# First feed-forward layer: 23 expert blocks of dispatched rows in place of eight experts on all rows

## The reference

```python
x = x + L0_gnn(adj, layernorm(x))    # max over a node's first 25 neighbours, then a dense layer
x = x + L0_ffn(layernorm(x))         # 8 experts, hidden 512, two used for each row
x = x + L1_gnn(layernorm(x), adj)    # attention, 8 heads, masked by adj
x = x + L1_ffn(layernorm(x))         # 6 experts, hidden 128

# L0_ffn
top_w, top_i = top_k(xf @ Wg + bg, 2); top_w = softmax(top_w)
w_dense = sum(one_hot(top_i, 8) * top_w[..., None], axis=1)
for e in range(8):
    h = gelu(xf @ W1[e] + b1[e])
    out = out + w_dense[:, e:e + 1] * (h @ W2[e] + b2[e])
```

## Time and profile before

| | us |
|---|---|
| median of three runs | 3452.06 |
| the profiled execution | 3442.75 |
| its span, first to last instruction | 3440.9 |
| time around the span | 1.85 |
| mean granted TensorE clock | 0.901 of 2.4 GHz |
| busy: PE, DVE, ACT, POOL | 2589.0, 1840.7, 1292.2, 837.9 |

### The profile page before, as it was taken

The page is one execution under the profiler, slowest core; times in us unless marked ns, Lnnn a source line. Parts: engine busy times, 40 slices in busy tenths (PEclk is TensorE's granted clock), DMA queues, the critical chain, the costliest instruction groups (busy, mean ns, idle before and its releaser), DMA issues.

```text
span 3440.9 us, 48188 instructions
## 1 busy us (share of the span) xinstructions
PE 2589.0 (75%) x16137; PEld 1525.4 (44%) x16137; DVE 1840.7 (53%) x5404; ACT 1292.2 (38%) x1959; POOL 837.9 (24%) x917
## 2 busy tenths in 40 slices
PE   0018626997699878996799779995799789986697
PEld 0015423654365445554465445643465346543044
DVE  3224335843686357744685358734694379124903
ACT  1004212354334643264335433372335432452054
POOL 3533530433041502242042402252043400000000
PEclk9988867998899988998899889997899899997598
DMA  5523524422532433332542343242442241004100
GB/s 132 59 27 65 50 38 88 75 38 32 105 64 37 46 58 89 45 52 24 105 75 33 37 77 79 39 53 22 104 75 37 33 82 36 2 1 74 37 2 7
DMA packets 106030, 183.66 MB, mean 53 GB/s; under 512 B 19935, under 2 KB 56188, under 8 KB 105724
## 3 DMA queue, kind: packets, MB, share of 16 engines
q0 software_dynamic: 25344, 51.96, 17.5%
q1 hardware_dynamic: 80380, 128.07, 15.2%
HBM read 158.59 MB, written 20.97 MB: 52 GB/s over the span
## 4 chain that ended last, share of the span: by engine, by line
DVE 35%; PE 30%; issue 18%; DMA 7%; DVEq 5%; ACT 3%; SPq 1%; ACTq 0%
DVE parts L1034 15%; PE PH L1293 5%; PE PA L1339 5%; PE PY L1354 4%; PE PA L1342 4%; PE PY L1304 4%; DMA parts_dram<-parts 4%; DMA xn<-in_x 2%; DVE res_n L940 2%; ACT HB L1165 2%; DVE G L823 2%; DVEq L744 2%; DVE score L791 2%; DVE top L795 1%; DVE xn L773 1%
## 5 line engine op out<-in xcount | busy, mean ns | idle before, releaser
L716 POOL DMA_INDIRECT G<-table,slot_idx x792 | 811.4, 1024 | 372.8 <-issue 372.8
L1158 ACT ACTIVATE HB<-PH,bias_T 128x512 f32<-128x512 f32 x512 | 351.3, 687 | 862.4 <-PE PH L1293 862.4
L1034 DVE CUSTOM_DVE_ANT_0 parts<-PA,mask 128x1024 bf16<-128x1024 f32 x512 | 627.0, 1225 | 19.8 <-issue 19.8
L1165 ACT ACTIVATE HB<-PA 128x1024 f32<-128x1024 f32 x512 | 496.0, 1020 | 364.8 <-PE PA L1342 364.6
L1304 PEld LDWEIGHTS PY<-W_sb,HB 128*128 128x128 f32 x4096 | 512.3, 195 | 134.4 <-issue 87.9
L1304 PE MATMUL PY<-W_sb,HB 128*128 128x128 f32 x4096 | 521.3, 279 | 65.2 <-DVE res_n L940 53.7
L1293 PE MATMUL PH<-XT,W_sb 128*128 128x512 f32 x1024 | 527.0, 630 | 17.4 <-ACT HB L1158 17.4
L1316 PE MATMUL PA<-KS,QS 96*128 96x512 bf16 x1024 | 342.1, 420 | 114.2 <-DVE MX L1034 58.7
L1339 PE MATMUL PA<-QS,KS 99*128 99x512 bf16 x1024 | 393.6, 384 | 11.2 <-ACT HB L1165 7.4
L1342 PE MATMUL PA<-identb,mask 128*128 128x128 bf16 x4096 | 397.1, 218 | 0.0
L594 POOL TENSOR_TENSOR pool_pad<-pool_pad 1x1 f32<-1x1 f32 x112 | 23.6, 210 | 1520.4 <-DVE slot_idx L803 1275.0
(11 more groups left out here) (156 smaller groups left out, 2270.1 us busy)
## 6 DMA issues: line engine op xcount, KB each, us to landing
adj_sb<-in_adj SPq DMA_DIRECT2D x64, 512.0 KB, 4.2
adjm<-in_adj SPq DMA_DIRECT2D x64, 512.0 KB
G<-table,slot_idx POOLq DMA_INDIRECT x792
parts_dram<-parts SPq DMA_DIRECT2D x16, 768.0 KB, 6.9
QS<-parts_dram SPq DMA_DIRECT2D x48, 256.0 KB, 8.3
KS<-parts_dram SPq DMA_DIRECT2D x48, 256.0 KB, 8.1
xn<-in_x SPq DMA_DIRECT2D x8, 512.0 KB, 13.1
table<-xn SPq DMA_DIRECT2D x8, 512.0 KB, 3.5
```

Source lines behind the costliest of these rows:

```text
L716: pool.indirect_dma_start(G[:, t % 2, s, :], None, table, bass.IndirectOffsetOnAxis(slot_idx[:, t, s:s + 1], axis=0), bounds_check=ROWS - ...
L1034: ins = dve.tensor_tensor_reduce(out=junk, in0=psum(ps, step)[:, :], in1=mask[:, t, :], scale=1.0, scalar=LOWEST, op0=ALU.add, op1=ALU.max ...
L1158: act.activation(HB[:, i % 2, c, :], psum(ps, step)[:, :], ACT.Gelu, bias=bias_T[:, e * HC + c:e * HC + c + 1]).then_inc(*emptied(ps, step))
L1165: act.activation(HB[:, kc % 2, 2 * pr:2 * pr + 2, :], psum(ps, key)[:, :].rearrange("p (h q) -> p h q", h=2), ACT.Exp, scale=float(D) ** - ...
```

## The change

Rows are sent to their experts. The new step `rank` (PE and DVE) counts, after the two best experts of graph b+2 are known, how many rows each expert has, and gives each of the 2048 (row, choice) pairs a place in a list sorted by expert, in which each expert starts at a multiple of 128. `disp` has POOL write the rows there, with 16 indirect DMAs of 128 rows (`sorted_x` in DRAM). The list has at most 23 blocks of 128 rows, and always 23 are computed.

In the next pass, SP loads the sorted rows in groups of four blocks (`xs`), and PE transposes them (`xT`). For each block, SP reads the block's expert number into a register and loads that expert's weights, 128 x 1028 numbers (526 KB), into a ring of three buffers (`wl`). PE makes four 128x128 products, ACT four Gelus of 128 columns (`up`), and PE four products (`dn`). `yc` and `yst` bring a group's result back to DRAM. When all are stored, `comb` fetches two result rows for each row with 16 indirect DMAs on POOL, and DVE adds them with their weights (16 additions). `comb` stands behind `mT` and ahead of `st`. The two units behind `mparts` and `mT` and the last unit at the end are gone, as are all `acc0`. Blocks start in `weave` when its count of TensorE time reaches 22. Ahead of everything, SP writes 23 DMAs of zeros into `sorted_x`. POOL now walks the list of steps too.

```diff
-ORDER0 = [(hf, e) for hf in range(2) for e in range(E0)]
 FINDS_EARLY = 10
+BLOCKS = 2 * TILES + E0 - 1
+PER_GROUP = 4
+GROUPS = (BLOCKS + PER_GROUP - 1) // PER_GROUP
+WRING = 3
+BLOCKS_FROM = 22.0
+WCOLS = 2 * HID0 + HC
...
-UNITS_MIDDLE = 2
-UNITS_LATE = 1
...
-        elif scores and (len(emptied) < 2 or emptied[-2] <= tensor or not main):
+        elif scores and (len(emptied) < 2 or emptied[-2] <= tensor or not main or tensor < BLOCKS_FROM):
...
-            if main[0][0] == "acc0":
-                vector = max(vector, tensor) + 1.15
-            else:
-                tensor += 0.87
+            tensor += PACE.get(main[0][0], 0.0)
             s.append(main.pop(0))
...
+    blocks = []
+    if unit:
+        blocks += [("xs", 0), ("xs", 1)] + [("wl", j) for j in range(WRING)] + [("xT", 0)]
+        for j in range(BLOCKS + 1):
+            if j < BLOCKS:
+                if j % PER_GROUP == 2 and j // PER_GROUP + 1 < GROUPS:
+                    blocks.append(("xT", j // PER_GROUP + 1))
+                    if j // PER_GROUP + 2 < GROUPS:
+                        blocks.append(("xs", j // PER_GROUP + 2))
+                blocks.append(("up", j))
+            if j > 0:
+                blocks.append(("dn", j - 1))
+                if j - 1 + WRING < BLOCKS:
+                    blocks.append(("wl", j - 1 + WRING))
+                g, last = group_of(j - 1)
+                if last:
+                    blocks += [("yc", g), ("yst", g)]
...
+    joined = [("comb",)] if unit else []
+    if not att:
+        s += spread(blocks, finds) if blocks else finds
+        s += joined
     else:
         cut = FINDS_EARLY if finds else 0
-        s += weave(scores, main, finds[:cut]) + second[:1] + experts0(middle[:1])
-        s += second[1:2] + experts0(middle[1:])
+        s += weave(scores, blocks, finds[:cut]) + second[:2] + joined
         s += spread(second[2:], finds[cut:])
...
-    s += late_down[0] + late_up[1]
...
+        s += [("ln", 3), ("t1",), ("r1",)]
...
-        chain += [("cha", 0), ("chb", 0), ("chc", 0)]
+        chain += [("cha", 0), ("rank",), ("disp",), ("chb", 0), ("chc", 0)]
...
+                    elif kind == "xs":
+                        g = step[1]
+                        if g == 0:
+                            sp.wait_ge(*at(ps, turn, "dsp"))
+                        if g >= 2:
+                            sp.wait_ge(*is_taken(ps, turn, ("xT", g - 2)))
+                        n = min(PER_GROUP, BLOCKS - g * PER_GROUP)
+                        sp.dma_start(rows_x[:, g % 2, 0:n, :],
+                                     sorted_v[:, g * PER_GROUP:g * PER_GROUP + n, :]).then_inc(S[f"xs{g % 2}"], 16)
+                    elif kind == "wl":
+                        j = step[1]
+                        if j >= WRING:
+                            g, last = group_of(j - WRING)
+                            if last:
+                                sp.wait_ge(*is_full(ps, turn, ("y", g)))
+                            else:
+                                sp.wait_ge(*at(ps, turn, "dn", ("dn", j - WRING)))
+                        if j >= WRING:
+                            sp.sem_inc(s_slot, 1)
+                        e = sp.value_load(expert[0:1, j:j + 1], min_val=0, max_val=E0 - 1)
+                        sp.dma_start(wbuf[:, j % WRING, :], wpack[e, :, :]).then_inc(S[f"wl{j % WRING}"], 16)
+                    elif kind == "yst":
+                        g = step[1]
+                        sp.wait_ge(*is_taken(ps, turn, ("y", g)))
+                        n = min(PER_GROUP, BLOCKS - g * PER_GROUP)
+                        sp.dma_start(sorted_yv[:, g * PER_GROUP:g * PER_GROUP + n, :],
+                                     rows_y[:, g % 2, 0:n * C].rearrange("p (q c) -> p q c", c=C)
+                                     ).then_inc(S[f"yst{g % 2}"], 16)
                     elif kind == "load_w":
+                        sp.wait_ge(s_zero, 16 * BLOCKS)
                         for dst, src in loads + late_loads:
                             sp.dma_start(dst, src).then_inc(s_w, 16)
...
+                    elif kind == "disp":
+                        pool.wait_ge(*at(ps, turn, "pos", ("rank",)))
                         held_by(pool, pool_pad, True)
...
+                        for j in range(2 * TILES):
                             pool.indirect_dma_start(
...
+                                sorted_x, bass.IndirectOffsetOnAxis(place[:, j:j + 1], axis=0),
+                                xn[:, j % TILES, :], None,
+                                bounds_check=BLOCKS * P - 1, oob_is_err=False).then_inc(S["dsp"], 16)
+                    elif kind == "comb":
+                        for i in range(2):
+                            g = GROUPS - 2 + i
+                            pool.wait_ge(*at(ps, turn, f"yst{g % 2}", ("yst", g)))
+                        held_by(pool, pool_pad, True)
+                        for j in range(2 * TILES):
+                            pool.indirect_dma_start(
+                                picked_y[:, j, :], None, sorted_y,
+                                bass.IndirectOffsetOnAxis(place[:, j:j + 1], axis=0),
+                                bounds_check=BLOCKS * P - 1, oob_is_err=False).then_inc(S["gy"], 16)
...
+            def place_rows(ps, turn, step):
+
+                key = ("tot",)
...
+            def join_experts(ps, turn, step):
+
+                dve.wait_ge(*at(ps, turn, "gy", step))
+                held_by(dve, dve_pad)
+                for i in range(2):
+                    for t in range(TILES):
+                        ins = dve.scalar_tensor_tensor(out=res_n[:, t, :], in0=picked_y[:, i * TILES + t, :],
+                                                       scalar=kept_w[:, i, t:t + 1], in1=res_n[:, t, :],
+                                                       op0=ALU.mult, op1=ALU.add)
+                    if i == 1:
+                        ins.then_inc(S["cmb"], 1)
+                    dve.drain()
 
...
+                    elif kind == "xT":
+                        g = step[1]
+                        n = min(PER_GROUP, BLOCKS - g * PER_GROUP) * P
                         act.wait_ge(*is_full(ps, turn, step))
-                        act.activation(HB[:, i % 2, c, :], psum(ps, step)[:, :], ACT.Gelu,
-                                               bias=bias_T[:, e * HC + c:e * HC + c + 1]).then_inc(*emptied(ps, step))
+                        act.activation(cols_x[:, g % 2, 0:n], psum(ps, step)[:, 0:n],
+                                       ACT.Copy).then_inc(*emptied(ps, step))
+                    elif kind == "up":
+                        j = step[1]
+                        act.wait_ge(*is_full(ps, turn, step))
+                        for c in range(HC):
+                            ins = act.activation(HB[:, 1, j % 2, c * P:(c + 1) * P],
+                                                 psum(ps, step)[:, c * P:(c + 1) * P], ACT.Gelu,
+                                                 bias=wbuf[:, j % WRING, 2 * HID0 + c:2 * HID0 + c + 1])
+                        ins.then_inc(*emptied(ps, step))
+                    elif kind == "yc":
+                        g = step[1]
+                        n = min(PER_GROUP, BLOCKS - g * PER_GROUP) * C
+                        act.wait_ge(*is_full(ps, turn, ("y", g)))
+                        if g >= 2:
+                            act.wait_ge(*at(ps, turn, f"yst{g % 2}", ("yst", g - 2)))
+                        act.activation(rows_y[:, g % 2, 0:n], psum(ps, ("y", g))[:, 0:n],
+                                       ACT.Copy).then_inc(*emptied(ps, ("y", g)))
                     elif kind == "st":
...
+                    elif kind == "rank":
+                        pe.wait_ge(*at(ps, turn, "pk", ("cha", 0)))
+                        chosen = pick[:, :, :, :].rearrange("p i t e -> p (i t e)")
+                        pe.wait_ge(*is_free(ps, turn, ("tot",)))
+                        pe.matmul(psum(ps, ("tot",))[:, 0:P], chosen, ones[:, :],
+                                  start=True, stop=True).then_inc(*filled(ps, ("tot",)))
...
+                    elif kind == "xT":
+                        g = step[1]
+                        pe.wait_ge(*at(ps, turn, f"xs{g % 2}", ("xs", g)))
                         pe.wait_ge(*is_free(ps, turn, step))
-                        pe.matmul(psum(ps, step)[:, :], W1_sb[:, e, c * P:(c + 1) * P], XT[:, half[hf]],
-                                         start=True, stop=True).then_inc(*filled(ps, step))
-                    elif kind == "down0":
-                        _, i, tt = step
...
+                    elif kind == "up":
+                        j = step[1]
+                        g, q = j // PER_GROUP, j % PER_GROUP
+                        if q == 0:
+                            pe.wait_ge(*is_taken(ps, turn, ("xT", g)))
+                        pe.wait_ge(*at(ps, turn, f"wl{j % WRING}", ("wl", j)))
```

(24 more changed lines are left out.)

285 lines of the change are left out of this document (184 added, 101 removed).

## The result

The changed kernel takes 3802.56 us (median of 4 runs, 3797.75 to 3815.26), the kernel before 3450.77 (4 runs). The ratio is 1.103, with an interval of 1.101 to 1.105. The forecast was 3670, with a range up to 3800; the loss is 352 us and not the 219 of the forecast. The profiled execution took 3815.26 us, its span 3813.5.

The account below looks back on a forecast made before the run. Scores, then tile 2's search and GpSimd's gathers, bound the kernel. Six full passes +168, attention-and-unit pass -9, pass without attention +49, start +11: +219 on 3442.75, 3662, plus 9.3 to the median: 3670 us, range 3500 to 3800.

Parts of the forecast that it names:

- What bounds the kernel: Full pass: scores bound by TensorE and VectorE, second half by tile 2's search and GpSimd's gathers through tile 7.
- Fetch and join: Between blocks' end and tile 2's gathers: uncovered, +52 us including 13.7 from the search's start to its first gather.
- Pass without attention and start: Dispatch +16 and end +33 make +49 us for that pass; zero stores and constants at the start add +11.
- Pass with attention and unit: Pass with attention and unit alone, without searches: blocks end at 127, net -9 us.
- First `up` at 46: First block's `up` in a full pass starts near 46 us after the first scores.
- Block period 4.2 us, blocks' end at 143: Full pass's scores: weight ring bounds 23 blocks at 4.2 us, 97 us in all, ending 143 us after first scores.
- round trip: Weight ring: from a buffer's release to its next load's landing, 5.5 us, of which 4.8 is landing.
- TensorE's part: Block period: TensorE's `up`, `dn` and a score pair, 2.45 us at full clock, 4.9 at half, taken as 2.9.
- Rival 2, half clock: TensorE at 1.2 GHz in the scores: period 5.1 us, blocks end at 163, total 3800 us; chance 0.15.
- Rival 1: Vector-bound scores: loads land near 3.2 us, blocks end at 124, total 3545 us; chance 0.15.
- Rival 3: Faster: TensorE is the true limit, fetch not in front of tile 2; -22 us per pass, about 3295; chance 0.09.
- Register load: SyncE's load of a block's expert number: 0.3 us, from VectorE's rows, inside the weight ring's round trip.

Follow-up runs that it names:

- g2: Changed kernel with each mask tile's load moved behind the fourth score of the tile before: 3864.99 us, 1.027 of the kernel before.
- e2: Changed kernel with five weight buffers in place of three: 3813.56 us, 1.010 of the kernel before.
- i1: Changed kernel with the later mask loads of g2 and no search step among the scores: 3885.77 us, 1.027 of the kernel before.
- i4: As g4, but with three weight buffers in place of five: 3881.16 us, 1.026 of the kernel before.
- g4: Changed kernel with five weight buffers, later mask loads, join just ahead of `take`, blocks started at 4 in place of 22: 3698.70 us, 0.981 of the kernel before.
- j2: g4 again on the last chip, where the kernel before takes 3435 us: 3432.60 us, 1.000 of the kernel before.

## Why the prediction was wrong, step by step

- **What bounds the kernel** (scores, then tile 2's search and GpSimd's gathers): right. Tile 3 follows tile 2 by the same 31 us, and the whole second half moved out with them.
- **Fetch and join**, +52: 48. Right.
- **Pass without attention and start**, +49 and +11: +58.6 together, by luck in part. The first gather of all came 4 us later (11 forecast), the dispatch added 10 (16) and the end 29 (33). Another 16 lie between the first and the last gathers of that pass, beside the blocks, where the forecast had nothing.
- **Pass with attention and unit**, -9: -4.4. Its blocks ended at +137, not +127.
- **First `up` at 46**: 49. It hid that a mask load stood ahead of the first weights (8 us sooner in g2).
- **Block period 4.2 us, blocks' end at 143**: this step failed, 5.35 and 172. 23 x 1.15 = 26.5 us per pass, which with 3 for the start and -4 for the fetch is the 25 us missing in each of six passes, 147 of the 154 us that the two traces differ from the sum. The form was right: half of the sum of a round trip and TensorE's part. The term mis-sized is the round trip: 5.5 us in the forecast (0.7 until the issue, 4.8 to land), 7.6 in the trace (1.8 and 5.8), and (7.6 + 3.1)/2 = 5.35 leaves TensorE's part near its 2.9.
- **What the forecast left out of the round trip**: it gave what disturbs the ring in a full pass 0.2 us per block (4.0 without search, 4.2 with); it was 0.9 (4.5 and 5.35). SyncE's queue, in which 7 of 20 loads stood for 2 us or more, was not in the forecast's round trip at all: of the 4.5 it has about 0.6 (100 to 86 us in g2). In the full passes of the first chip, 181 of the 268 us that TensorE waited ahead of `up` stand at the 35 loads behind a mask tile's load, and 117 of them where gathers ran as well; how much each of the two would give back alone there was not run, and stays open.
- **Why a median misled**: the forecast's 4.8 is near the median landing of 5.0, and with the medians (0.8 + 5.0) the same form gives 4.5. TensorE takes the blocks in order and the loads come in order, so a late one (10.1, 11.8 us) is paid for, and an early one gives little back. The mean carries the tail.
- **Rival 2, half clock**, gave nearly the time measured, for a reason that did not hold. It took the low clock as a cause; e2 took 26 us off the blocks at nearly the same clock, and in i1 the clock rose as the waits went. A part of it was real: behind the long waits shown above the products ran at 1.2 GHz, 2.07 us for an `up` in place of 1.13. Its own terms, (5.5 + 4.9)/2, give a period of 5.2 and not the 5.1 that it used.
- **Rival 1** (blocks done at 124): in reach with the early start and the later mask loads (+119 in i4, +109 in g4, +90 in j2). **Rival 3** needed the fetch out of the chain, with tile 2's gathers at 145 and 22 us off each pass: j2 has them at +150 and wins 6 per pass on average, since the end of the pass grew.
- **Register load**: the 184 of SyncE took 268 ns in the median (262 to 905), near VectorE's 300:

```profile
L683 SPq TENSOR_LOAD <-expert x184: 262/268/905, 288.1 to 3324.0; - x184
```

  The Trainium skill (DMA: Bandwidth & Descriptors, "Latency and other measured facts") gives a floor of about 600 ns; the trace does not agree, and the measurement decides.

## What to carry to other kernels

Size a ring by its disturbed round trip: take from the trace the mean and the longest landing beside the traffic that will run there, not the median, and read in the issuing queue what stands ahead of each load and what that waits for. A wait of one engine for data it needs once per step is paid by every engine whose work is queued behind it, so a move that takes work off a matrix engine can lengthen the stretch. Before believing a low clock as a cause, look for the waits ahead of it. When an edit shortens a stretch, look which waits went: a large gain can be another cause's, as in i1.

## What the runs showed of the hardware

- On the chips of four groups the kernel before took 3769 to 3786 us, on two others 3435 to 3452. The one trace of it there shows the difference in the passes with searches and indirect transfers (TensorE's same instructions, 166 us for 133); the last two passes, without them, were equal to 1% (347.2 and 271.5 us against 348.7 and 270.4).
- 16 indirect reads of 128 rows of 512 B landed 22.9 us after the first was issued, 1.4 us each, against 27.0 for the gathers of the earlier trace rows.
- Two things that each cost little cost much together: a 526 KB weight load landed in 4.2 us on average alone, 5.3 behind a mask tile's load, 6.8 beside gathers and 12.6 with both.
